# Three relational graph layers on one core: each product of rows and weights formed before the sum over counts

## The reference, cut to what matters

```python
def rgcn_conv(h, src, dst, edge_type, w_rel, w_root, bias):
    xw = jnp.einsum('nd,rde->rne', h, w_rel)
    msg = xw[edge_type, src]
    ...
    inv = jnp.where(count > 0, 1.0 / jnp.maximum(count, 1.0), 0.0)
    msg = msg * inv[dst, edge_type][:, None]
    agg = jax.ops.segment_sum(msg, dst, num_segments=num_nodes)
    return agg + h @ w_root + bias
h = jnp.concatenate([x, node_emb[node_type]], axis=-1)
h = jax.nn.relu(rgcn_conv(h, src, dst, edge_type, w_rel1, w_root1, b1))
h = jax.nn.relu(rgcn_conv(h, src, dst, edge_type, w_rel2, w_root2, b2))
h = jax.nn.relu(rgcn_conv(h, src, dst, edge_type, w_rel3, w_root3, b3))
```

## Time and profile before

| | us |
|---|---|
| median of 3 runs | 1882.32 |
| lowest, highest | 1880.95, 1883.13 |
| the profiled execution, own time | 1880.43 |
| its span in the trace | 1878.3 |
| TensorE busy in it | 1774.6 (94%) |
| VectorE, ScalarE, GpSimd busy | 912.6, 468.2, 689.7 |

### The profile page before, as it was taken

One profiled execution on the slowest core, in us unless ns is written; L12 is line 12 of the kernel. 1 busy time (PEld: TensorE's weight loads), 2 busy tenths in 40 slices (PEclk: granted clock), 3 DMA queues, 4 the chain that ended last, 5 costly groups with the idle time before them and its releaser, 6 DMA issues.

```text
span 1878.3 us, 26804 instructions
## 1 busy us (share of the span) xinstructions
PE 1774.6 (94%) x10673; PEld 1636.1 (87%) x10673; DVE 912.6 (49%) x1915; ACT 468.2 (25%) x890; POOL 689.7 (37%) x428
## 2 busy tenths in 40 slices
PE   6799999999999988899899999999999999998999
PEld 6699988898988987898377899998999999997899
DVE  8983243317853569957497651223322252226321
ACT  3543222203222138934132300110101111113210
POOL 1027554562344520050020234435534353334554
PEclk9899999999999999899899989999999999999999
DMA  2002221233111210014000011111211121111122
GB/s 83 1 26 59 78 68 46 95 106 127 59 51 51 68 45 15 1 43 131 10 30 1 20 50 50 40 50 61 68 43 43 51 68 46 48 43 52 59 61 74
DMA packets 41727, 99.59 MB, mean 53 GB/s; under 512 B 10354, under 2 KB 11991, under 8 KB 41618
## 3 DMA queue, kind: packets, MB, share of 16 engines
q1 hardware_dynamic: 37828, 87.87, 15.3%
q10 hardware_dynamic: 3790, 10.14, 1.6%
HBM read 96.08 MB, written 1.92 MB: 52 GB/s over the span
## 4 chain that ended last, share of the span: by engine, by line
PE 73%; DVE 11%; ACT 5%; PEld 3%; issue 2%; POOL 1%; PEldq 0%; DVEq 0%; ACTq 0%; POOLq 0%
PE banks L2194 9%; PE bank L2194 9%; PE banks L2195 8%; PE banks L2196 8%; PE bank L2195 8%; PE bank L2196 8%; PE bank L2292 6%; PE banks L2292 5%; PE banks L2733 2%; PE bank L2733 2%; ACT prob L1050 1%; PE banks L2582 1%; ACT lesser L1051 1%; PEld bank L2426 1%; DVE edge_scores L1764 1%
## 5 line engine op out<-in xcount | busy, mean ns | idle before, releaser
L746 POOL TENSOR_TENSOR w_hi<-raw,ones_r 128x768 fp32r<-128x768 f32 (+1 forms) x192 | 293.0, 1526 | 1129.5 <-PE bank L2196 448.4
L749 POOL TENSOR_TENSOR w_lo<-raw,w_hi 128x768 fp32r<-128x768 f32 (+1 forms) x192 | 372.1, 1938 | 15.1
L2194 PE MATMUL bank<-w_hi,xT_hi 128*125 128x384 f32 (+2 forms) x558 | 188.6, 338 | 2.8 <-issue 1.0
L2196 PE MATMUL bank<-w_hi,xT_lo 128*125 128x384 f32 (+2 forms) x558 | 187.0, 335 | 0.0
L2195 PE MATMUL bank<-w_lo,xT_hi 128*125 128x384 f32 (+2 forms) x558 | 187.0, 335 | 0.0
L2194 PE MATMUL banks<-w_hi,xT_hi 128*125 128x384 f32 (+2 forms) x482 | 166.7, 346 | 3.1 <-DVE acc L2131 1.6
L2195 PE MATMUL banks<-w_lo,xT_hi 128*125 128x384 f32 (+2 forms) x482 | 166.2, 345 | 0.0
L2196 PE MATMUL banks<-w_hi,xT_lo 128*125 128x384 f32 (+2 forms) x482 | 166.0, 344 | 0.0
L2194 PEld LDWEIGHTS bank<-w_hi,xT_hi 128*125 128x125 f32 x558 | 104.2, 187 | 8.8 <-issue 2.4
L2154 DVE SCALAR_TENSOR_TENSOR acc<-banks,small,acc 125x384 f32<-125x384 f32 (+1 forms) x48 | 29.6, 634 | 166.9 <-PE banks L2196 166.9
L2195 PEld LDWEIGHTS bank<-w_lo,xT_hi 128*125 128x125 f32 x558 | 104.2, 187 | 2.6
(11 more groups left out here) (534 smaller groups left out, 4011.9 us busy)
## 6 DMA issues: line engine op xcount, KB each, us to landing
raw<-wa SPq DMA_DIRECT2D x92, 384.0 KB, 3.0
raw<-wc SPq DMA_DIRECT2D x76, 384.0 KB, 3.0
raw<-wb SPq DMA_DIRECT2D x28, 448.0 KB, 3.2
w_rows<-w_in ACTq DMA_DIRECT2D x1, 3072.0 KB, 12.7
bias<-bias_in ACTq DMA_DIRECT2D x6, 384.0 KB
w_first<-w_in ACTq DMA_DIRECT2D x1, 2304.0 KB, 8.8
w_down<-w_down_in SPq DMA_DIRECT2D x8, 288.0 KB, 5.3
w_up<-w_up_in SPq DMA_DIRECT2D x1, 2304.0 KB, 11.7
```

The costliest lines, as they stand in the source:

```text
L746: pool.tensor_tensor(w_hi[:, k, 0:width], raw[:, k, 0:width], ones[:, 0:1].to_broadcast([P, width]), ALU.mult).then_inc(S("unit_high"), 1)
L749: pool.tensor_tensor(w_lo[:, k, 0:width], raw[:, k, 0:width], f(w_hi[:, k, 0:width]), ALU.subtract).then_inc(S("unit_split"), 1)
L2194: pe.matmul(dst, l_hi, r_hi, start=start, stop=False)
L2196: return pe.matmul(dst, l_lo, r_hi, start=False, stop=stop)
```

## The change

All of it is in the seventh block, its three relational layers, and the places that feed them.

1. For each relation and half of the columns, `through` multiplies the layer's own transposed rows with the relation's weights (as the root does); ScalarE and VectorE split the result straight from PSUM into `through_hi[c]` and `through_lo[c]`, 5 tiles each; `relation_sum` then sums them by counts (5 matmuls of high, 5 of low, for each target tile). VectorE scales and adds as before. `gather`, and the split of node rows, are gone here.
2. `RELATION_STEPS` puts the next `through` between a `through` and its own `sum`.
3. The embedding is no longer part of the rows. Its three rows, transposed (128 by 4), are multiplied with the first weight slice (3 matmuls), split into a high and a low row of `type_rows[c]`, and one matmul for each tile with a one-hot `types_K` of 36 rows adds them to the group.
4. Degrees: in the first layer two columns of ones stand ahead of `through_hi[0]`, so the sum of the first half gives the degree in its first column.
5. relu of layers one and two moves into the split behind the transposes. A tile is transposed two tiles behind its last sum; the last two behind the first two tiles of the next layer's root product, whose first 4 slices go tile by tile.
6. In `g3c` the second half of the root product is moved to the end: its last 4 slices go tile by tile, and each tile's last sum follows at once, with a transpose for `f3` two tiles behind.

The weights are put in the new order on the host. The core of the diff:

```diff
+RELATION_STEPS = (("through", 0, 0), ("through", 0, 1), ("sum", 0, 0), ("through", 1, 0), ("sum", 0, 1), ("through", 1, 1),
+                  ("sum", 1, 0), ("through", 2, 0), ("sum", 1, 1), ("through", 2, 1), ("sum", 2, 0), ("sum", 2, 1))
+HEAD_UNITS = 2
...
-            act.wait_ge(*E("g3_emb_low", NT))
-            nodes_high("g3_xn", D1, acc, "g3a_nodes_high")
...
+                    for n in range(NT):
+                        i = 2 * NT * r + NT * c + n
+                        await_group(act, key + "_through", i)
+                        act.activation(through_hi[c][:, n, 2 - 2 * c:2 - 2 * c + width],
+                                       bank(key + "_through", i)[0:TN, 0:width], ACT.Copy).then_inc(S(key + "_high"), 1)
...
-                    if i == 2 * NT + 6 + n:
-                        dve.wait_ge(*E("g3a_nodes_high", n + 1))
-                        TT(nm_lo[:, n], acc[:, n], f(nm_hi[:, n]), ALU.subtract).then_inc(S("g3a_nodes_low"), 1)
...
+            def through_low(key, r, c):
+                width = DOWN[key][1]
+                for n in range(NT):
+                    i = 2 * NT * r + NT * c + n
+                    dve.wait_ge(*E(key + "_high", i + 1))
+                    TT(through_lo[c][:, n, 0:width], bank(key + "_through", i)[0:TN, 0:width],
+                       f(through_hi[c][:, n, 2 - 2 * c:2 - 2 * c + width]), ALU.subtract).then_inc(S(key + "_low"), 1)
...
+            def through(key, label, feed, c, first, tile_ready=None, turn=None, after=None):
...
+                if typed:
...
+                    close(three(dst[0:4, 0:cw], emb_parts[:, 0], emb_parts[:, 1], w_hi[:, u % RING, w], w_lo[:, u % RING, w],
+                                True, True), "g3a_types", at)
...
+                for j, n in order:
...
+                    last = three(bank(label, i)[0:TN, 0:cw], xT_hi[:, k, at], xT_lo[:, k, at], w_hi[:, u % RING, w],
+                                 w_lo[:, u % RING, w], k == 0, j == kt - 1 and not typed)
...
+                    if j == kt - 1:
+                        if typed:
...
+                            last = pe.matmul(bank(label, i)[0:TN, 0:cw], types_K[:, at], type_rows[c][:],
+                                             start=False, stop=True)
...
+            def relation_sum(key, r, c, turn=None, tiles=range(NT)):
+                cw, first = DOWN[key][1], 2 * NT * r + NT * c
+                counted = 2 if key == "g3a" and c == 0 else 0
+                begin = 2 - 2 * c - counted
+                for n in tiles:
+                    dst = open_bank(key + "_sum", first + n)
+                    at = slice(n * TN, (n + 1) * TN)
+                    for s in range(NT):
+                        if n == 0:
+                            pe.wait_ge(*E(key + "_high", first + s + 1))
+                        pe.matmul(dst[0:TN, 0:counted + cw], rel[:, r, s, at],
+                                  through_hi[c][:, s, begin:begin + counted + cw], start=s == 0, stop=False)
+                    for s in range(NT):
+                        if n == 0:
+                            pe.wait_ge(*E(key + "_low", first + s + 1))
+                        last = pe.matmul(dst[0:TN, counted:counted + cw], rel[:, r, s, at], through_lo[c][:, s, 0:cw],
+                                         start=False, stop=s == NT - 1)
...
+                    else:
+                        through(key, "g3c_root", 0, 1, NT,
+                                after=lambda n: relation_sum("g3c", RELS - 1, 1, turns["f3"], (n,)))
```

More of the change, by code:

```diff
@@ L308, in plan_groups @@
     several("R", R_DRAINS, "R_taken")
[L309 to L321, removed]
+    several("g3a_hT", 2 * NT, "g3a_hT_low")
@@ L352, in families @@
         family(half, [("g0", 24), ("f0", 24), ("g1a", 12), ("g1b", 12), ("f1", 16), ("g2p", HEADS),
[L353 to L356, removed]
+                      ("g3a", 2 * NT * RELS), ("g3b", 2 * NT * RELS), ("g3c", 2 * NT * RELS), ("f3", 24)])
+        family("nodes_" + half, [("g1", NT), ("g1b", 2 * NT)])
+    family("T_pad", each("g0_x f0_x f1_x g2_x f2_x f3_x", 2))
+    for layer in "g0_x f0_x f1_x g2_x f2_x f3_x".split():
         table[layer + "T_pad"] = table.pop(layer + "_T_pad")
@@ L2041, in _ @@
             TT(hidden_T[:], hidden_T[:], own_slots[:], ALU.mult).then_inc(S("f2_masked"), 1)
-            for n in range(NT):
-                await_group(dve, "g3_emb", n)
-                dve.tensor_copy(acc[:, n, D:D1], bank("g3_emb", n)[0:TN, 0:TYPE_DIM]).then_inc(S("g3_emb_low"), 1)
             for c in range(2):
@@ new lines, in _ @@
+            await_group(dve, "R", R_DRAINS - 1)
+            for i in range(2):
+                dve.memset(f(type_rows[i][:]), 0.0).then_inc(S("g3a_clear"), 1)
+            dve.memset(f(through_hi[0][:, :, 0:2]), 1.0).then_inc(S("g3a_clear"), 1)
+            for key, k, following in (("g3a", KD, ("g3b", K1)), ("g3b", K1, ("g3c", KD)), ("g3c", KD, None)):
+                width = DOWN[key][1]
+                for n in range(0 if key == "g3a" else NT - LOW_LAG, NT):
+                    turned_parts(key, k, n)
+                if key == "g3a":
+                    types_low(0)
@@ L2695, in _ @@
             slots_turned("f2_hiddenT", slot_hidden, "f2_hidden_read")
-            pe.wait_ge(*E("type_hot", 1))
-            pe.wait_ge(*E("emb_loaded", 16))
-            for n in range(NT):
-                dst = open_bank("g3_emb", n)
-                close(pe.matmul(dst[0:TN, 0:TYPE_DIM], type_hot[:, n * TN:(n + 1) * TN], emb[:], start=True, stop=True),
-                      "g3_emb", n)
             pe.wait_ge(*E("f2_bias_full", 16))
@@ new lines, in turn_relations, with turn @@
+            def turn_relations(before, key, k):
+                def turn(n):
+                    pe.wait_ge(*E(before + "_acc", 2 * NT * RELS + NT + n + 1))
+                    turn_tile(key + "_hT", acc, k, n)
+                return turn
+            pe.wait_ge(*E("types_hot", 1))
+            pe.wait_ge(*E("emb_split", 1))
+            transposes("g3a_hT", acc, KD, "g3_xn")
+            turns = {"g3b": turn_relations("g3a", "g3b", K1), "g3c": turn_relations("g3b", "g3c", KD), "f3": turn_behind("f3")}
@@ L2762, in _ @@
+            for n in range(NT - TURN_LAG, NT):
+                turns["f3"](n)
             expert_layer("f3", 12, 2)
```

304 lines of the change are left out of this document (210 added, 94 removed).

## The result

The changed kernel takes 1863.2 us (median of 4 runs, 1862.4 to 1865.9) where the kernel before takes 1882.5 (1880.95 to 1883.1): a ratio of 0.9901, 95% interval 0.9884 to 0.9919, so 19 us or 1.0% faster. The forecast was 1836.5, the range 1828 to 1848: the sign was right, less than half of the gain came. The profiled execution of the changed kernel is the slowest of its four, 1865.9 us, with a span of 1864.2 and a mean granted clock of 0.971.

A forecast was written before the change was run, and what follows sets the result against it. TensorE, with work in 94% of the span, was taken as the bound. The terms -14.5, -16.2, -6.8, -1.4, -4.6, +1 and -3.3 sum to -45.8 us, giving 1834.6 profiled and 1836.5 median; range 1828 to 1848.

The forecast's parts named there:

- columns: TensorE's matmuls in the three layers, priced by streamed columns: -17.4 us, or -14.5 with layer one's root taken out.
- degrees: Degree matmuls before relations 0 and 2 of layer one, and slow gathers behind them, go away: -16.2 us.
- counts: TensorE's stall in edge tile 22, waiting for ScalarE to read a bank, goes: -6.8 us, lower bound 4.1.
- root of layer one: Second half of layer one's root product: the wait still ends at 1083.3, fewer matmuls follow: -1.4 us.
- at nothing: Work said to cost no time beside TensorE's: splits of `through`, POOL's weight units, embedding instructions, small DMAs, moved last root half.
- joints, with the changes: Two joints between layers, transposes spread among sums and root: -4.6 us; changing between transposes and matmuls: +1 us.
- end of `g3c`: Before the router: last transposes start about 4.3 us after the last sum instead of 7.6: -3.3 us.
- 8 x 5 type rows: Layer one's 40 type matmuls, counted among the 448-column matmuls at 0.204 us each.
- VectorE has the same work before it as before, so this stays at 1083.3: Layer one's root, second half: VectorE's bank read keeps its time; TensorE comes sooner and waits some 3.5 us.
- a granted clock of 1.00 all through: Sign expected in the new trace: TensorE's granted clock stays at 1.00 throughout the layers.
- rival 2: Lower clock in the new blocks after thin 4-column matmuls and the drain, eight times: 22 us, 1858; chance 0.04.
- Rival 1: Stalls move: counts wait taken up by VectorE's one-hot rows, joints and `g3c` end keep their time: 1847; chance 0.13.

The follow-up runs named there:

- runs 1 to 5: The changed kernel with TYPE_ROWS at 128, 64, 100, 96 and 65 in place of 36: 1847.0, 1862.2, 1847.9, 1846.7 and 1847.9 us.
- run 9: The kernel before without its 75 degree matmuls and their readers, reciprocal degrees set to a constant 0.2: 1865.6 us.
- run 10: The kernel before with ScalarE's five `nm_hi` copies and VectorE's five subtractions moved from the counts to behind the last counts: 1876.5 us.
- run 7: The changed kernel with VectorE's last three `settle_relations` moved behind the additions of the first half of layer one's root: 1854.5 us.
- run 6: The changed kernel with VectorE's `last_relation` moved behind the second block's types, ahead of the third relation's: 1854.1 us.
- run 8: The changed kernel with type rows padded to 128, `last_relation` later and the last three `settle_relations` later, all together: 1829.3 us.

## Why the prediction was right and wrong

The sum of the prediction by its own terms, against what the runs and the two traces show:

| term | predicted | shown |
|---|---|---|
| columns | -14.5 | holds but for the type rows: products and sums start every 0.204 and 0.176 us, the matmuls with 4 stationary columns every 0.205 |
| the 40 type matmuls within it | 0.204 us each | 0.60 us each: 16.2 us more (runs 1 to 5) |
| degrees | -16.2 | -16.7, in the trace -15.8 (run 9) |
| counts | -6.8 | -6.7 (traces; run 10) |
| root of layer one | -1.4, a wait of 3.5 | a wait of 5.2 and a clock of 0.50 for 6.8 us; without them the kernel is 8.7 faster (run 7) |
| `types_low(2)` behind `last_relation` | at nothing | 9.1 us (run 6) |
| joints, with the changes | -4.6 + 1 | -4.5: beyond its matmuls' pace PE spent 2.2 and 2.3 us at the two joints before and nothing now; a change costs nothing that shows |
| end of `g3c` | -3.3, transposes 4.3 us behind the last sum | 5.2 us behind it, so -2.4 |

**First wrong step: the price of the type matmuls.** "8 x 5 type rows" went into the 448-column count at the pace of equal matmuls. I wrote that two prices have no row of their own and named the 4 stationary columns, which cost just what I took. The other unpriced thing, 36 rows between full tiles, I did not name. The trace of before has such a step all the same, in another block: a matmul of 4 rows (L2381) between matmuls of 128, at a granted clock of 1.00. PE's timeline of the kernel before:

```profile
332.45 0.30 PE L2196 MATMUL banks<-xT_hi,w_lo 128*128 128x314 f32 x1
332.68 0.40 PE L2381 MATMUL bank<-cT,pat 4*128 4x312 f32 x1
333.01 0.41 PE L2194 MATMUL bank<-xT_hi,w_hi 128*128 128x312 f32 x1
333.26 0.31 PE L2195 MATMUL bank<-xT_lo,w_hi 128*128 128x312 f32 x1
```

From 332.45 to 333.26 three starts take 0.81 us where 0.144 each gives 0.43. The small tile costs 0.38 us more than its columns, and forty at that price are 15 us: the term could have been read from before and was not.

**Second: the cover that I gave VectorE.** "At nothing" stand the splits of `through`, and for those it was right. `types_low` is in no term: I looked at what it issues (0.6 us), not at what stands ahead of it in VectorE's queue. Before, `last_relation` is needed by relation 2 alone. Now `types_low(2)` stands behind it, and TensorE asks for that in relation 0.

**Third: "VectorE has the same work before it as before, so this stays at 1083.3".** It has the same instructions and takes longer over them: the wait ends 34.7 us behind the first transposes of the layer, in place of 31.4. DVE's timeline in the last counts of the changed kernel, two of the 21 instructions, and POOL's beside them:

```profile
1063.66 0.63 DVE L2137 SCALAR_TENSOR_TENSOR rel<-r_rounded,rel 125x456 fp32r<-125x456 f32 x1
1064.21 2.12 DVE L2129 SCALAR_TENSOR_TENSOR r_taken<-r_rounded,r_taken 125x456 f32<-125x456 f32 x1
```

```profile
1064.11 1.72 POOL L789 TENSOR_TENSOR w_hi<-raw,ones_r 128x896 fp32r<-128x896 f32 x1 [108.34 <-PE banks L2289]
1065.91 2.40 POOL L792 TENSOR_TENSOR w_lo<-raw,w_hi 128x896 fp32r<-128x896 f32 x1
```

The same kind of instruction takes 0.63 us, and 2.12 when POOL is splitting weights. Of the 21 instructions 6 are stretched so before and 8 after, every one of the 14 overlaps an instruction of POOL, and no short one lies within one; POOL makes 6 instructions in that time before, with pauses of 1.8 and 1.9 us, and 8 now, with one of 0.8, since the first weight units come free closer together (the embedding's slice takes 3 matmuls now, and the next three slices go tile by tile). So the 21 take 22.2 us before and 25.4 now. In `last_relation` 7 of 10 are stretched, and the ten take 18.3 us where 0.8 each would make 8. The Trainium skill has a rule that would do this (SBUF — State Buffer, section SBUF: two separate sides): VectorE and GpSimd share one pair of ports as an exclusive lock, which a VectorE instruction with two SBUF inputs takes against a GpSimd instruction that reads SBUF. This trace agrees: the splits of `through` (L2196, one input in PSUM, 448 columns) take 0.625 us each, the four that lie within an instruction of POOL as well as the 19 that touch none. No run here took POOL's work away, so that POOL is the cause rests on these overlaps; that VectorE's queue ahead of the additions is the cause of the wait is shown by run 7.

**Fourth: "a granted clock of 1.00 all through".** It fell in or just behind both new waits. A wait of 5.2 us was priced at its length by me, and the kernel was 8.7 us faster without it and what was slow behind it; without the one of 2.9 us it was 9.1 faster. How long the clock stays down is not set by the wait alone: the same wait of 2.9 us brought 13.7 us of 0.50 in the changed kernel and 10.2 in run 7. The waits of 1.6 us before and at the start of a sum (0.3 us) brought no fall. I had only asked whether thin work would lower the clock (rival 2), and the 4-column matmuls, its cause, ran at full pace wherever no wait was near.

Taken together: the forecast holds a wait of 3.5 us at the root, so without any wait it is -49.3. The three losses of layer one, as they are together in the traces (run 8), give 32.1 back, the end of `g3c` 0.9; degrees, counts and joints were off by 0.4, 0.1 and -0.9. That makes -49.3 + 32.1 + 0.9 + 0.4 + 0.1 - 0.9 = -16.7. From the first matmul of the counts to the router's first, the part that the prediction is about, the two traces differ by 17.7 us (787.8 and 770.2), so 1 us is left open there. Behind the router, in code that is the same, another 1.3 us went (154.3 us before, 153.0 after); that and the rest of the 19.2 are of the size by which executions of one kernel differ.

Rival 1, that stalls move, was the right kind at the wrong places: I looked for them where VectorE released TensorE before, and the counts and the joints gave all that was forecast. The new ones arose where the change put a new consumer behind an old queue.

## What to carry to other kernels

Price a new matmul by its row count too: where tiles of up to 64 rows alternate with full ones, pad them with zeros to more than 64, which cost nothing that shows here and saved 16 us. Look for the price of a new kind of step in the whole trace, not only in the layers that change. When a part that an engine must serve is moved earlier, read that engine's whole queue ahead of it, and lengthen each two-input VectorE instruction for the POOL work that now falls beside it. Waits of 2.9, 4.1 and 5.2 us of a busy TensorE cost 9.1, 6.7 and 8.7 us here, 1.6 to 3.1 times their length, so look for the queue order that removes such a wait before counting columns.

## What the runs showed of the hardware

- A matmul of 36 or 64 rows between matmuls of 128 rows costs 0.40 us more than one of 65, 96, 100 or 128 rows (1863.2 and 1862.2 us against 1847.9, 1846.7, 1847.9 and 1847.0 for 40 of them). In the 36-row trace 0.10 of it shows before the tile, 0.19 in it and 0.10 to 0.12 behind it. A 4-row matmul of 312 columns between matmuls of 128 rows costs 0.38 us more in the trace of before. By the Trainium skill (TensorE: Matmul & The Clock Gate, section LDWEIGHTS (loading the stationary operand)) a weight load goes by its columns and not by its rows; the load's own record agrees (0.180 us with 36 rows, 0.185 with 128). So the extra 0.40 us is not the length of the load; what it is no run here shows.
- A VectorE instruction with two SBUF inputs and 125x456 elements takes 0.62 us alone; 11 took 2.0 to 2.6 in the two traces, each beside POOL's split of a weight unit.
